# The root of 1024 moves from rstd into gamma in a routed two-layer adapter kernel

## The chip, the cores and the metric

The kernel runs on one core of a Trainium2 chip. The metric is the device time of one execution, in microseconds (us). The kernel before was timed in three runs: 2746.89 us is their median, 2745.69 the lowest and 2746.93 the highest.

## The reference

128 items of 128 rows by 1024 columns go through two adapter layers. Each item carries a role (0, 1 or 2) that picks its weights:

```
h = x @ W_down[role] + b_down[role]          # 1024 -> 512
h = gelu(h)                                  # exact gelu
y = x + h @ W_up[role] + b_up[role]          # 512 -> 1024, residual
mean, var over the 1024 columns of y
out = (y - mean) * rsqrt(var + 1e-5) * gamma[role] + beta[role]
```

The second layer does the same on the result of the first, with its own weights, gamma and beta. All of it is in fp32.

## The kernel before, in words

**Order of the items.** The kernel first sorts the items by role on the chip, so that items with the same adapter lie side by side, and pairs them: 65 pairs in each layer, 130 in all (a role with an odd number of items fills its last pair up). A pair's number is `c`. Where a pair is the first with a new adapter, new weights, biases, gamma and beta are fetched, and the weights are split in a high and a low part. The inputs hold two roles, so this happens twice in each layer: gamma and beta are fetched four times (`gains` on SyncE, lines 309 and 310).

**The step.** Every engine walks through steps `i`; in step `i` it works on several pairs at once. TensorE does the down products of pair `i` (`down`, line 517) and the seven up products of pair `i-3` (`product`, line 529), numbered 0 to 6 here as p0 to p6, in the fixed order p0, down, p1, down, ... There are 90 matmuls of 512 columns in a full step. The up product is written with sums and differences of blocks: GpSimd forms sums of the hidden blocks of pair `i-2` (`sums`, lines 470 to 475, tile `cs`), and VectorE adds the banks onto the rows in `xt` (`onto`, line 950; `last_onto`, line 958).

**Normalization.** For a pair whose rows are complete, ScalarE squares and sums (line 704), VectorE adds that up (`variance`, line 973; there H times the variance, with H = 1024, comes out, because the sum isn't divided), and GpSimd's `norm` makes `rstd` of it in two operations on a 128 by 2 tile: the power -0.5 (line 445), then, after a wait for its own first result, times the root of 1024 (line 448). Meanwhile VectorE's `scale` (line 981) computes (x + nmean) * gamma in place over 128 by 1024, once for each of the two items. ScalarE's `normal` (line 712) multiplies that by `rstd`, and GpSimd's `shift` (line 462) adds beta. Then the rows are stored. For the very last pair `norm_last` (lines 454 and 456) does one item at a time, and VectorE's `finish` (line 996) multiplies by rstd and adds beta in one operation.

**What sets the order.** Each engine's list is written by hand and runs in order; semaphores tie them. `count(eng, s, p, per, plus)` waits until semaphore `s` has `per*c + plus`. Two orders matter here. On GpSimd a step is: `sums(i-2)`, then, if pair `i-4` has a new adapter, `take_gb` (wait until gamma and beta have landed), then the semaphore `s_cg` goes up, then `norm(i-4)`, `shift(i-4, 0)`, `shift(i-4, 1)`. VectorE's `scale` waits for `s_cg`, and behind `scale` on VectorE stand, in this order, the first `last_onto` of the step (it reads the bank of p3, and TensorE's p5, which writes the same bank anew, waits for it through `s_v`), `transpose_x` in the second layer, the second `last_onto` (which waits for p4), and the rest of the step. On ScalarE `normal(i-4, 0)` stands ahead of `high_x(i+1, 0)` (line 644, the split of the next pair's x), `gelu(i, 0)` and more; each `normal` waits for `s_rs`.

The high and low parts of new weights are made by ScalarE (lines 598 and 611) and VectorE (`low_wd`, line 841; `low_wu`, line 860), in the steps just before the new gamma is first used.

## Time and profile before

| What | Value |
|---|---|
| Median of three runs | 2746.89 us (2745.69 to 2746.93) |
| Span of the profiled execution, first to last instruction | 2744.8 us |
| TensorE (PE) busy | 2683.5 us, 98% |
| VectorE (DVE) busy | 2206.7 us, 80% |
| ScalarE (ACT) busy | 1666.1 us, 61% |
| GpSimd (POOL) busy | 1385.3 us, 50% |
| Instructions | 54370 |

The profiler gives the span of the profiled execution; no other time of that execution is listed, and the span is what its rows add up to. "Idle before" is time in which the engine waited ahead of an instruction, and the arrow names what ended it; "issue" means that the profile shows nothing that the engine waited for. PEclk is the clock that TensorE was granted, 1.00 for 2.4 GHz and 0.50 for 1.2 GHz. Names such as L448 are lines of the kernel.

### The profile page before, as it was taken

Reading aid. Unit: us, or ns where it says so; the run is one execution under the profiler, and the core shown is the slowest. Engines: PE = TensorE matmul, PEld = TensorE weight load, DVE = VectorE, ACT = ScalarE, POOL = GpSimd, SP = SyncE. Lnnn points to the kernel's source line nnn. Section 1 sums busy time; section 2 is a strip of 40 time slices with the busy share of each in tenths; the row PEclk is TensorE's granted clock in tenths of the full one; section 3 lists DMA queues with packets and bytes.
Section 4 is the critical chain, followed back from the end, with each engine's and each line's share of the span. In section 5 each row is a group of like instructions: output and inputs, shape, how many; then the busy total and the mean of one; then the engine's idle time right before and its main releaser. Section 6 shows DMA issues by size and latency. Waiting matters only on the chain.

```text
span 2744.8 us, 54370 instructions
## 1 busy us (share of the span) xinstructions
PE 2683.5 (98%) x11714; PEld 2203.5 (80%) x11714; DVE 2206.7 (80%) x3357; ACT 1666.1 (61%) x2905; POOL 1385.3 (50%) x1050
## 2 busy tenths in 40 slices
PE   8999999999999999999989999999999999999997
PEld 6888888887888888888768888888778888888885
DVE  6777777779777777777898888888888888888886
ACT  5656656666666665665656566665666565665664
POOL 1455555455555555555545454554444455545545
PEclk9999999999999999999999999999999999999998
DMA  6656656666666666656766566666766665766654
GB/s 226 212 194 213 211 200 214 201 228 231 215 214 202 207 207 205 214 200 224 233 200 225 185 220 206 205 214 202 240 197 214 200 222 188 226 202 203 215 191 148
DMA packets 360590, 573.35 MB, mean 209 GB/s; under 512 B 40144, under 2 KB 239952, under 8 KB 359248
## 3 DMA queue, kind: packets, MB, share of 16 engines
q1 hardware_dynamic: 358704, 554.14, 61.6%
q10 hardware_dynamic: 1440, 15.47, 1.6%
q14 instruction: 434, 3.56, 0.5%
q8 instruction: 12, 0.20, 0.0%
HBM read 364.97 MB, written 204.47 MB: 207 GB/s over the span
## 4 chain that ended last, share of the span: by engine, by line
PE 86%; DVE 6%; issue 5%; ACT 1%; POOL 1%; DVEq 1%; DMA 0%; ACTq 0%; POOLq 0%; SPq 0%
PE pD L517 45%; PE bX L529 23%; PE bZ L529 17%; DVE wul L860 1%; DVE xt L958 1%; DVE hl L940 1%; DVE xT L911 1%; DVE xt L950 1%; DVE xt L981 0%; ACT xh L644 0%; DVE wdl L841 0%; DVE hT L925 0%; DVE xl L918 0%; POOL cs L470 0%; POOL cs L472 0%
## 5 line engine op out<-in xcount | busy, mean ns | idle before, releaser
L517 PE MATMUL pD<-wdh,xh 128*128 128x512 f32 x2080 | 812.4, 391 | 15.4 <-DVEq L902 15.4
L462 POOL TENSOR_TENSOR xt<-xt,cgb 128x1024 f32<-128x1024 f32 x258 | 630.8, 2445 | 359.4 <-ACT xt L712 359.4
L517 PE MATMUL pD<-wdh,xl 128*128 128x512 f32 x2080 | 811.3, 390 | 0.0
L517 PE MATMUL pD<-wdl,xh 128*128 128x512 f32 x2080 | 811.2, 390 | 0.0
L470 POOL TENSOR_TENSOR cs<-hT 128x256 f32<-128x256 f32 x130 | 151.6, 1166 | 902.9 <-DVE hT L925 902.9
L704 ACT ACTIVATE pC<-xt,nmean 128x512 f32<-128x512 f32 x520 | 358.7, 690 | 246.0 <-DVE nmean L966 236.8
L712 ACT ACTIVATE xt<-xt,rstd 128x1024 f32<-128x1024 f32 x258 | 296.3, 1149 | 316.3 <-POOL rstd L448 312.7
L517 PEld LDWEIGHTS pD<-wdh,xh 128*128 128x128 f32 x2080 | 391.6, 188 | 99.7 <-DVEq L902 12.4
L517 PEld LDWEIGHTS pD<-wdh,xl 128*128 128x128 f32 x2080 | 391.7, 188 | 82.1
L517 PEld LDWEIGHTS pD<-wdl,xh 128*128 128x128 f32 x2080 | 391.8, 188 | 81.3
L529 PE MATMUL bX<-wuh,hh 128*128 128x512 f32 x1040 | 408.0, 392 | 17.4 <-DVEq L902 9.5
L529 PE MATMUL bX<-wuh,hl 128*128 128x512 f32 x1040 | 406.0, 390 | 0.0
L529 PE MATMUL bX<-wul,hh 128*128 128x512 f32 x1040 | 405.9, 390 | 0.0
L694 ACT ACTIVATE hh<-cs 128x512 fp32r<-128x512 f32 x260 | 163.6, 629 | 371.8 <-PE bX L529 283.6
L940 DVE TENSOR_TENSOR hl<-cs,hh 128x512 fp32r<-128x512 f32 x260 | 298.9, 1168 | 104.0 <-issue 97.6
L981 DVE SCALAR_TENSOR_TENSOR xt<-xt,nmean,cgb 128x1024 f32<-128x1024 f32 x260 | 327.8, 1301 | 2.5 <-POOLq L483 2.4
L529 PE MATMUL bZ<-wuh,hh 128*128 128x512 f32 x780 | 307.4, 394 | 12.6 <-issue 7.6
L529 PE MATMUL bZ<-wul,hh 128*128 128x512 f32 x780 | 305.0, 391 | 0.0
L529 PE MATMUL bZ<-wuh,hl 128*128 128x512 f32 x780 | 304.9, 391 | 0.0
L950 DVE TENSOR_TENSOR xt<-bX,xt 128x512 f32<-128x512 f32 x260 | 178.8, 688 | 147.8 <-PE bX L529 146.6
L958 DVE SCALAR_TENSOR_TENSOR xt<-bX,xt 128x512 f32<-128x512 f32 x260 | 176.9, 680 | 97.9 <-PE bX L529 97.7
L445 POOL TENSOR_TENSOR rstd<-var,mhalf 128x2 f32<-128x2 f32 x129 | 218.1, 1691 | 68.5 <-DVE var L973 64.9
(106 smaller groups left out, 3817.4 us busy)
## 6 DMA issues: line engine op xcount, KB each, us to landing
xq<-in_xB SPq DMA_DIRECT2D x130, 512.0 KB, 3.6
htok<-hg SPq DMA_DIRECT2D x260, 256.0 KB, 2.9
hq<-htok SPq DMA_DIRECT2D x1040, 64.0 KB, 2.2
xt<-in_x SPq DMA_DIRECT2D x130, 512.0 KB, 4.3
mid<-xt SPq DMA_DIRECT2D x130, 512.0 KB, 3.8
xq<-mid SPq DMA_DIRECT2D x520, 128.0 KB, 3.2
xt<-mid SPq DMA_DIRECT2D x130, 512.0 KB, 4.4
out<-xt SPq DMA_DIRECT2D x128, 512.0 KB, 3.0
```

The costliest lines, as they stand in the source:

```text
L445: eng.tensor_tensor(rstd[:, n:n + 2], var[:, n:n + 2], mhalf[:, 0:1].broadcast_to([128, 2]), ALU.pow)\
L462: eng.tensor_tensor(xt[:, k, :], xt[:, k, :], cgb[:, 1, :], ALU.add).then_inc(s_o, 1)
L470: eng.tensor_tensor(cs[:, 0, :], b1, b2, ALU.add).then_inc(s_S, 1)
L517: last = eng.matmul(pD[e][:, :], a[:, e, 128 * k:128 * k + 128], w[:, k, :], start=False, stop=(k == 7 and n == 2), skip_group_check=True)
L529: last = eng.matmul(bank[:, :], a[:, left, 128 * c:128 * c + 128], w[:, n, c, :], start=(start and c == 0 and m == 0), stop=(c == 1 and m ...
L694: eng.activation(dst, src, ACT.Copy).then_inc(s_hh, 1)
L704: eng.activation(junk[:, :], xt[:, u.slot(e), K * m:K * m + K], ACT.Square, bias=nmean[:, n:n + 1], accum_out=ssq[:, b, m, e:e + 1]).then_ ...
L712: eng.activation(xt[:, k, :], xt[:, k, :], ACT.Copy, scale=rstd[:, n:n + 1]).then_inc(s_z, 1)
L940: eng.tensor_tensor(blocks, src, high.bitcast(fp32), ALU.subtract).then_inc(s_hl, 1)
L950: eng.tensor_tensor(half(u, e, m), bank[:, :], half(u, e, m), ALU.add).then_inc(s_v, 1)
L958: eng.scalar_tensor_tensor(out=half(u, e, m), in0=bank[:, :], scalar=1.0, in1=half(u, e, m), op0=ALU.mult, op1=ALU.add, accum_out=ys[:, b, ...
L981: eng.scalar_tensor_tensor(out=xt[:, k, :], in0=xt[:, k, :], scalar=nmean[:, n:n + 1], in1=cgb[:, 0, :], op0=ALU.add, op1=ALU.mult).then_i ...
```

## The change

`rstd` is no longer multiplied by the root of 1024. Instead gamma is multiplied by it once, when a new gamma has landed: GpSimd's `take_gb` multiplies the whole 128 by 1024 tile by the number, and waits until that is done before `s_cg` goes up. The counts of `s_rs` are halved, since each pair now gives one signal where it gave two, and the tile and the memset that held the root are gone.

```
-        rooth = sb("rooth", [128, 1])
+        s_gr = sem("s_gr")
...
-            eng.memset(rooth[:, :], float(H) ** 0.5).then_inc(s_id, 1)
             eng.memset(zero[:, :], 0.0).then_inc(s_zero, 1)
-            eng.wait_ge(s_id, 2)
+            eng.wait_ge(s_id, 1)
...
             def take_gb(p):
-                eng.wait_ge(s_gb, pg.next() * 32 + 32)
+                c = pg.next()
+                eng.wait_ge(s_gb, c * 32 + 32)
+                eng.sem_inc(s_seen, 1)
+                eng.tensor_scalar(cgb[:, 0, :], cgb[:, 0, :], float(H) ** 0.5, None, ALU.mult).then_inc(s_gr, 1)
+                eng.wait_ge(s_gr, c + 1)
                 eng.sem_inc(s_seen, 1)

             def norm(p):
                     eng.tensor_tensor(rstd[:, n:n + 2], var[:, n:n + 2], mhalf[:, 0:1].broadcast_to([128, 2]), ALU.pow)\
                        .then_inc(s_rs, 1)
-                    count(eng, s_rs, p, 2, 1)
-                    eng.tensor_tensor(rstd[:, n:n + 2], rstd[:, n:n + 2], rooth[:, 0:1].broadcast_to([128, 2]), ALU.mult)\
-                       .then_inc(s_rs, 1)

             def norm_last(p, e):
                 eng.tensor_tensor(rstd[:, n:n + 1], var[:, n:n + 1], mhalf[:, 0:1], ALU.pow).then_inc(s_rs, 1)
-                count(eng, s_rs, p, 2, 2 * e + 1)
-                eng.tensor_tensor(rstd[:, n:n + 1], rstd[:, n:n + 1], rooth[:, 0:1], ALU.mult).then_inc(s_rs, 1)
...
             def normal(p, e):
-                    count(eng, s_rs, p, 2, 2)
+                    count(eng, s_rs, p, 1, 1)
...
             def finish(u, e):
-                count(eng, s_rs, u, 2, 2 * e + 2)
+                count(eng, s_rs, u, 1, e + 1)
```

## Rows read from the trace of the kernel before

**Rows 1.** The page: busy time, share of span, instructions; then the chain's shares by engine.

```profile
PE 2683.5 (98%) x11714; PEld 2203.5 (80%) x11714; DVE 2206.7 (80%) x3357; ACT 1666.1 (61%) x2905; POOL 1385.3 (50%) x1050
...
PE 86%; DVE 6%; issue 5%; ACT 1%; POOL 1%; DVEq 1%; DMA 0%; ACTq 0%; POOLq 0%; SPq 0%
```

**Rows 2.** Windows: length, then busy us of each engine, granted clock, DMA share, GB/s.

```profile
1003.00:1023.40 20.40, 20.40 (x92) 16.89 (x91) 15.21 (x25) 12.55 (x23) 11.03 (x8) 1.00 0.63 208
...
668.80:699.20 30.40, 23.15 (x92) 17.73 (x91) 25.08 (x34) 17.89 (x31) 13.74 (x9) 0.94 0.45 151
```

**Rows 3.** Waits: who waited for whom, us in total, times, the longest.

```profile
ACT xt L712 <- POOL rstd L448: 312.7, 115, 7.3
...
ACT hh L694 <- issue: 26.8, 4, 7.5
```

**Rows 4.** Groups of GpSimd's lines: count, busy us, mean ns, idle before.

```profile
L445 POOL TENSOR_TENSOR rstd<-var,mhalf 128x2 f32<-128x2 f32 x129 | 218.1, 1691 | 68.5 <-DVE var L973 64.9 <-DMA cgb<-in_be 0.4
...
L448 POOL TENSOR_TENSOR rstd<-rstd,rooth 128x2 f32<-128x2 f32 x129 | 78.5, 609 | 10.1
...
L430 POOL MEMSET xt<- 128x1024 f32 x1 | 1.0, 952 | 0.0
```

**Rows 5.** Timeline of a plain step: start us, us, engine, line, what.

```profile
1013.00 2.48 DVE L981 SCALAR_TENSOR_TENSOR xt<-xt,nmean,cgb 128x1024 f32<-128x1024 f32 x2
1013.11 1.74 POOL L445 TENSOR_TENSOR rstd<-var,mhalf 128x2 f32<-128x2 f32 x1 [0.41 <-DVE var L973]
...
1014.92 0.61 POOL L448 TENSOR_TENSOR rstd<-rstd,rooth 128x2 f32<-128x2 f32 x1
...
1016.80 2.41 POOL L462 TENSOR_TENSOR xt<-xt,cgb 128x1024 f32<-128x1024 f32 x1 [1.26 <-ACT xt L712]
...
1018.26 2.03 DVE L918 TENSOR_TENSOR xl<-xq,xh 128x1024 fp32r<-128x1024 f32 x1
```

**Rows 6.** The chain that ended last, steps 30 and 31: start us, us, what.

```profile
619.60 0.63 POOL rstd L448
```

**Rows 7.** Timeline, steps 29 to 31.

```profile
600.95 2.40 POOL L462 TENSOR_TENSOR xt<-xt,cgb 128x1024 f32<-128x1024 f32 x1 [1.10 <-ACT xt L712]
...
602.03 2.40 DVE L841 TENSOR_TENSOR wdl<-rwd,wdh 128x1024 fp32r<-128x1024 f32 x1
...
632.15 1.06 ACT L644 ACTIVATE xh<-xq 128x1024 fp32r<-128x1024 f32 x1 [1.04 <-issue]
```

**Rows 8.** Timeline, step 34, which first uses the second gamma.

```profile
708.77 0.74 POOL L475 TENSOR_TENSOR cs<-hT,cs 128x256 f32<-128x256 f32 x1
...
708.91 2.87 DVE L981 SCALAR_TENSOR_TENSOR xt<-xt,nmean,cgb 128x1024 f32<-128x1024 f32 x2 [0.73 <-POOLq L483]
711.71 0.68 DVE L958 SCALAR_TENSOR_TENSOR xt<-bZ,xt 128x512 f32<-128x512 f32 x1
...
712.80 0.39 PE L529 MATMUL bZ<-wuh,hh 128*128 128x512 f32 x1
```

**Rows 9.** Timeline, step 99, which first uses the fourth gamma.

```profile
2067.60 2.47 DVE L981 SCALAR_TENSOR_TENSOR xt<-xt,nmean,cgb 128x1024 f32<-128x1024 f32 x2
2069.99 0.68 DVE L958 SCALAR_TENSOR_TENSOR xt<-bZ,xt 128x512 f32<-128x512 f32 x1
...
2071.73 0.39 PE L529 MATMUL bZ<-wuh,hh 128*128 128x512 f32 x1
```

**Rows 10.** Timeline, step 69, which first uses the third gamma.

```profile
1436.03 2.48 DVE L981 SCALAR_TENSOR_TENSOR xt<-xt,nmean,cgb 128x1024 f32<-128x1024 f32 x2 [0.17 <-POOLq L483]
1438.43 0.69 DVE L958 SCALAR_TENSOR_TENSOR xt<-bZ,xt 128x512 f32<-128x512 f32 x1
...
1441.08 0.39 PE L529 MATMUL bZ<-wuh,hh 128*128 128x512 f32 x1
```

**Rows 11.** Timeline, step 4, which first uses the first gamma.

```profile
88.29 0.69 DVE L958 SCALAR_TENSOR_TENSOR xt<-bX,xt 128x512 f32<-128x512 f32 x1 [1.39 <-PE bX L529]
```

**Rows 12.** The chain that ended last, its last microseconds: start us, us, what.

```profile
2736.62 0.20 POOL rstd L456
```

More of the change, by code:

```diff
@@ L567, in _ @@
         def _(eng):
-            eng.wait_ge(s_id, 2)
+            eng.wait_ge(s_id, 1)
             eng.activation(gelu_set[:, :], mhalf[:, :], ACT.Gelu)
```

## The prediction

> **What bounds the kernel now.** I read the page first. TensorE is busy 98% of the span and makes up 86% of the chain that ended last [rows 1]. The windows show what that means: in a plain step TensorE is busy all of the 20.40 us, at full clock, while VectorE works 15.2, ScalarE 12.6 and GpSimd 11.0 (first of [rows 2]). 130 such steps are 2652 us of the span of 2744.8. The other 93 us are the start, the drain of the last steps, and the steps in which an adapter changes: step 33 lasts 30.4 us with VectorE busy for 25.1 of them (second of [rows 2]). So an edit moves the time only there; in a plain step it must first use up the slack of its engine.
>
> The waits come next. ScalarE waits 312.7 us in 115 places for line 448, the operation that goes [rows 3]. That looks like a large sum, but these waits lie beside TensorE's 20.40 us. The chain of waits says where it is otherwise: in the stretch from 600 to 660 us the chain leaves TensorE and passes through line 448, at 619.60 and once more at 638.56, 0.63 and 0.62 us each (the first of these two stands in [rows 6]), and at the very end it passes through line 456 [rows 12]. At the other adapter changes it runs over VectorE and no operation on rstd.
>
> **What goes: the second operation on rstd.** 129 operations of 609 ns are 78.5 us of GpSimd [rows 4]. In the plain step the power ends at 1013.11 + 1.74 = 1014.85, the multiplication runs from 1014.92 to 1015.53 [rows 5]; without it rstd is ready 0.68 us sooner, in every step. ScalarE's `normal` follows, and GpSimd's add of beta (1016.80) follows that. This also clears VectorE's way: its 128x1024 subtraction began at 1018.26 and ended at 1020.29, 1.08 us after the add's end at 1019.21 [rows 5]; the one at 602.03 ended at 604.43, 1.08 us after an add that ended at 603.35 [rows 7]. VectorE stood until GpSimd's add was through, so an add that is 0.68 us earlier frees VectorE as much earlier. In a plain step all this is cover: TensorE takes 20.40 us with or without it, and I count 126 or so steps at nothing. If that cover were gone, it would be up to 0.68 us a step.
>
> Around the first big adapter change it does count. Three links are in line: the add that held up the weight work of step 29 (602.03), and line 448 in steps 30 and 31. Each is worth 0.68. One may be lost: at 632.15 ScalarE waited 1.04 us for something that the profile doesn't name [rows 7]; TensorE or a transfer. If the advance ends there, only the last 0.68 is left; if not, all three are: 2.04. I take two: **-1.36 us** (bounds -0.68 and -2.04). At the third and fourth changes (around 1400 and 2030 us) the chain doesn't pass rstd: nothing.
>
> At the end line 456 takes 0.20 us in the chain, with a handover of 0.07 as between 1014.85 and 1014.92 [rows 12, 5]: **-0.27 us**. The memset that goes and the wait for one signal less stand ahead of a start that waits for the items' roles: nothing.
>
> **What comes: gamma times the root, four times.** It is one operation of 128x1024 with one tensor as input, on GpSimd, in front of `s_cg`. VectorE's two `scale` operations wait for that, and `last_onto` and TensorE's p5 stand behind. No row shows such an operation. From below, the memset of the same size took 0.95 us [rows 4]; from above, the add with two tensor inputs took 2.41 [rows 5]. I take 1.2, near the memset, since one of the add's two operands is missing. With three handovers of 0.07, say 0.2 to 0.25, it puts 1.45 us between the end of `sums` and `scale`.
>
> On one rule the Trainium skill goes further: GPSIMD Engine Reference, section 3.1, puts a body of one or two operations per element at 1.03 cycles an element, and a body with two inputs at 2.6. By that the new operation is at the memset's end of the bracket, an estimated 0.9 us at that page's 1.2 GHz, and the sum below would be 0.6 us lower.
>
> Step by step:
> - Step 34: `sums` ended at 708.77 + 0.74 = 709.51. `scale` began at 708.91, since the signal had been sent as soon as the last sum was issued [rows 8]. Now it begins at 709.51 + 1.45 = 710.96. The pair took 2.87 beside GpSimd's sum, alone it takes 2.48 [rows 5], so `last_onto` begins at 711.71 - 0.39 + 2.05, which is 1.65 us later. TensorE's p5 began at 712.80, 0.42 after `last_onto` ended (711.71 + 0.68 = 712.39). VectorE enters this step 0.68 earlier, since its subtraction in step 33 follows an add of beta as above. 1.65 - 0.68 - 0.42 = 0.55, taken as **+0.6 us**. Bounds: 0.3 with 0.95 us, 2.4 with 2.41 us and no advance.
> - Step 99: `scale` at 2067.60 moves by 1.45; `last_onto` ended at 2070.67, p5 began at 2071.73, so 1.06 is slack [rows 9]: **+0.4 us**. Bounds 0.1 and 1.6.
> - Step 69: `scale` at 1436.03 had waited for gamma and beta; `last_onto` ended at 1439.12, p5 began at 1441.08: 1.96 of slack against 1.45 [rows 10]: nothing; 0.7 with 2.41.
> - Step 4: `last_onto` had ended and VectorE sat idle for 1.39 us until p4 was through at 88.29 [rows 11]; p5 begins one group of six matmuls later (20.40 / 15 = 1.36), so there are some 2.6 us of slack against at most 1.45: nothing, with 2.41 too (2.66).
>
> On GpSimd the power of that step comes 1.2 us later and the multiplication that goes gives half of it back. The adds of beta behind it move with it, and nothing on SyncE's queue but these two stores; ScalarE's later work in the step does wait for `normal`, but step 34's stretch up to the next step's down products has over a microsecond of room in the plain pattern. I leave it at nothing.
>
> **The sum**, against the profiled span: -1.36 - 0.27 + 0.6 + 0.4 = -0.6, so 2744.8 becomes 2744.2. The median of the runs stands 2.1 us above the span (2746.89 against 2744.8), and I keep that: **2746.3 us**.
>
> **Rivals.**
> - *Gamma's operation is dear.* It costs what the add costs, 2.41 us, and holds `s_cg` for as long. Then steps 34, 99 and 69 give 2.4 + 1.6 + 0.7 = 4.7; with the least gain, -0.68 - 0.27, it is +3.8: 2750.7 us, slower than before. Two steps pay for each microsecond, so the change loses from some 1.5 us for the operation on. For it speaks that all of GpSimd's known long operations run at that pace; against it that the memset doesn't.
> - *A first call that waits.* An operation of a kind that GpSimd hasn't run before may stand until its code is there. The nearest row is ScalarE's longest wait without a cause, 7.5 us [rows 3]. In step 4 that is 1.45 + 7.5 less the 2.6 of slack, so +6.4: 2752.7 us; if it happened at each of the four, 7.5 more in each of three, 2775. The Trainium skill names such a thing: GPSIMD Engine Reference, section 2.1, says that the first call to a freshly loaded kernel pays a load of about 6 us that no instruction shows. Nothing in the trace before shows such a gap, so I hold it for unlikely.
> - *More is freed than counted.* All three links count (-2.04), the operation takes 0.95 us (+0.3 + 0.1), and with shorter stalls TensorE keeps its clock in one stretch more. In step 33 the granted clock was 0.94 [rows 2], which is 0.06 x 30.4 = 1.8 us lost. Sum: -2.04 - 0.27 + 0.4 - 1.8 = -3.7: 2743.2 us.
> - *The power takes the time over.* The multiplication ended at 1015.53, with VectorE's second `scale` (1013.00 + 2.48 = 1015.48) [rows 5]. If rstd were held by `scale` and not by the multiplication, the gains in steps 29 to 31 would be 0, and the sum +1.2 + 0.4 - 0.27: 2748.2 us. Against it: the power ended at 1014.85, before `scale` did.
>
> **Chances and range.** The forecast, within a microsecond and a half: 0.60; the dear operation 0.14; the first call 0.04; more freed 0.12; the power takes over 0.10. The range reaches from the third rival to close to the first, 2743.4 to 2750.2. A measurement can tell about 0.2% of this kernel, 5.5 us, from no change. Only the first call lies past that on the slow side, and a sum of small misses: 0.05. On the fast side 0.03. The rest, 0.92, is no change.
>
> **What would show it.** Right: no line 448; ScalarE's wait for rstd now names line 445 and is some 0.68 x 115 = 78 us shorter than 312.7; plain steps of 20.40 us as before; four operations of about 1.2 us on cgb; a wait of about 2 us of VectorE's `scale` for GpSimd in step 34; step 34 longer than 20.40 us by half a microsecond; steps 30 to 33 together shorter by 1.4; the last finish 0.27 sooner. Wrong: a plain step that isn't 20.40 us, a gamma operation above 1.5 us, or a stall on TensorE at steps 4 or 69. What I can't see is how the pauses without a named cause on VectorE and ScalarE fall once the timing shifts; they could move the sum by a microsecond or two either way.

## The result and the profile after

The changed kernel takes 2752.12 us, the median of 20 runs (2749.16 to 2753.77). The kernel before takes 2746.64 us beside it, also 20 runs (2745.48 to 2748.84). The ratio is 1.0018, with a 95% interval of 1.0012 to 1.0024: slower by 5.5 us, where 0.6 us faster was forecast. The profiled execution has a span of 2750.7 us (own time 2752.52) against 2744.8. At 0.18% that is just inside what the prediction called no change, and 1.9 us above the upper end of its range.

First the page: busy time of each engine, share of the span, instructions; then the shares of the chain that ended last. It answers to [rows 1].

```profile
PE 2687.6 (98%) x11714; PEld 2208.4 (80%) x11714; DVE 2157.7 (78%) x3357; ACT 1675.1 (61%) x2905; POOL 1318.5 (48%) x922
...
PE 85%; DVE 6%; issue 6%; POOL 1%; ACT 1%; DVEq 1%; DMA 0%; ACTq 0%; POOLq 0%; SPq 0%
```

GpSimd has 128 instructions fewer: 129 multiplications in the steps, two for the last pair and one memset are gone, and four operations are new. It works 67 us less, not 78.5, mainly since the four new ones bring 11.1. The groups of its lines, with count, busy time, mean ns and the idle time before, show both (they answer to [rows 4]):

```profile
L448 POOL TENSOR_TENSOR rstd<-var,mhalf 128x2 f32<-128x2 f32 x129 | 219.1, 1698 | 64.5 <-DVE var L971 59.5 <-POOL cgb L440 1.2
...
L440 POOL TENSOR_SCALAR cgb<-cgb 128x1024 f32<-128x1024 f32 x4 | 11.1, 2780 | 0.2 <-DMA cgb<-in_be 0.2
```

The second row is the news: gamma's operation takes 2.78 us. The prediction took 1.2 and had 2.41 as its upper bound.

The windows of a plain step, of step 33, and of the steps 34 and 99, which first use the second and the fourth gamma (length, busy time of each engine, granted clock, DMA share, GB/s; compare [rows 2]):

```profile
1003.00:1023.40 20.40, 20.40 (x92) 16.89 (x91) 14.28 (x25) 12.69 (x24) 10.42 (x7) 1.00 0.64 218
670.08:699.65 29.57, 22.94 (x91) 17.61 (x90) 24.47 (x33) 17.93 (x31) 13.64 (x8) 0.94 0.51 167
699.80:724.10 24.30, 22.30 (x91) 17.96 (x90) 17.77 (x30) 13.00 (x23) 13.12 (x8) 0.93 0.74 237
2061.10:2084.50 23.40, 21.16 (x91) 16.64 (x90) 18.20 (x29) 11.53 (x21) 11.89 (x8) 1.00 0.71 216
...
716.00:719.40 3.40, 3.40 (x10) 2.63 (x9) 2.99 (x4) 3.40 (x6) 2.27 (x2) 0.50 0.22 87
```

The plain step is what it was, 20.40 us, all of it TensorE's. Step 33, counted from its first matmul to that of the next step, is 0.6 us shorter (29.72 after 30.36). Step 34 now lasts 24.3 us and step 99 23.4. In step 34 TensorE is idle for 2.0 us (24.30 less 22.30). It is also busy longer than in a plain step, because its granted clock stands at 0.50 for 3.4 us, from 716.0 on: at the 1.2 GHz level the same matmuls take 1.7 us more. TensorE had stood still until 715.56, just before that.

The timeline of step 34 tells the stall from its cause to its effect (start, duration, engine, line, what, and in brackets the idle time before it with what ended it; compare [rows 8]):

```profile
708.77 0.74 POOL L473 TENSOR_TENSOR cs<-hT,cs 128x256 f32<-128x256 f32 x1
...
709.47 2.78 POOL L440 TENSOR_SCALAR cgb<-cgb 128x1024 f32<-128x1024 f32 x1
...
712.41 2.48 DVE L979 SCALAR_TENSOR_TENSOR xt<-xt,nmean,cgb 128x1024 f32<-128x1024 f32 x2 [4.23 <-POOLq L481]
...
714.81 0.69 DVE L956 SCALAR_TENSOR_TENSOR xt<-bZ,xt 128x512 f32<-128x512 f32 x1
...
715.56 0.50 PE L527 MATMUL bZ<-wuh,hh 128*128 128x512 f32 x1 [2.00 <-DVE xt L956]
...
2071.54 2.78 POOL L440 TENSOR_SCALAR cgb<-cgb 128x1024 f32<-128x1024 f32 x1
...
2074.48 2.48 DVE L979 SCALAR_TENSOR_TENSOR xt<-xt,nmean,cgb 128x1024 f32<-128x1024 f32 x2 [2.84 <-POOLq L481]
...
2077.62 0.50 PE L527 MATMUL bZ<-wuh,hh 128*128 128x512 f32 x1 [1.77 <-DVE xt L956]
```

Read from the top: GpSimd's last sum, gamma's operation, VectorE's `scale` 0.16 us after that ends, then `last_onto`, then TensorE's p5. It is the chain the prediction named, and the last three rows are the same in step 99, with a stall of 1.77 us. The chain that ended last (start, duration, what) now runs over gamma's operation; before, it stayed on TensorE all through this step:

```profile
709.47 2.79 POOL cgb L440
...
715.56 2.61 PE bZ L527 x6
```

The waits (who waited for whom, total, times, longest) show the other half, which did what was forecast. They answer to [rows 3]:

```profile
ACT xt L710 <- POOL rstd L448: 239.8, 114, 6.6
...
DVE xt L979 <- POOLq L481: 13.5, 6, 4.2
```

ScalarE waits 72.9 us less for rstd. Nearly all of that lies in plain steps and is worth nothing. The second row was 2.4 us before, and its 4.23 is the wait in step 34.

To see where the time is, I cut every profile at the first matmul of chosen steps. The stretches below are us, counted from the traces; the last column is the span. Kernels of the experiments stand in the same table.

```
                    to 0  0-3   4     5-29   30-33 34    35-68  69    70-98  99    100-129 130-  span
before              17.21 58.64 20.40 510.00 92.94 20.42 707.88 20.40 609.53 21.11 612.76 53.55 2744.8
e7_prices           28.98 60.45 20.40 510.00 92.39 20.71 708.43 20.40 608.11 21.94 613.30 54.30 2759.4
e13_more_prices     29.06 58.74 20.40 510.00 92.91 20.47 707.89 20.40 608.23 21.89 613.23 53.63 2756.9
e2_gamma_only       16.91 59.56 20.49 510.00 92.31 25.43 708.26 21.40 608.65 23.21 613.09 53.20 2752.5
after               16.90 60.44 20.49 510.00 91.96 24.31 708.41 21.05 607.56 23.42 612.19 54.01 2750.7
after_again         16.93 59.47 20.49 510.00 91.46 23.17 707.87 21.28 608.09 23.33 612.75 52.76 2747.6
e1_no_gamma         16.93 59.74 20.40 510.00 91.66 20.40 708.33 20.40 608.37 21.64 612.03 53.78 2743.7
e11_two_ops         16.89 60.37 20.40 510.00 91.97 20.97 709.10 20.40 607.25 22.58 612.35 53.05 2745.3
e3_half             16.93 60.28 20.40 510.00 91.90 21.41 708.73 20.40 607.14 23.10 612.59 54.16 2747.0
e6_two_inputs       17.01 60.39 20.40 510.00 91.94 21.81 708.21 20.40 607.94 23.55 612.46 53.09 2747.2
e4_twice            16.92 60.33 25.06 510.00 91.48 27.47 708.53 27.10 607.96 28.70 612.00 52.78 2768.3
e10_root_on_dve     16.94 58.81 20.40 510.00 91.33 20.40 708.88 20.40 609.17 22.46 613.46 52.06 2744.3
e8_dve_gamma        17.57 59.73 20.40 510.75 91.41 20.40 708.76 20.40 610.71 22.44 613.43 53.88 2749.9
e14_root_in_square  16.95 58.99 20.40 510.00 91.51 20.40 708.38 20.40 607.38 21.53 612.37 53.95 2742.3
```

From before to after, the steps 4, 34, 69 and 99 cost 0.09 + 3.89 + 0.65 + 2.31 = 6.9 us. Steps 30 to 33 give back 1.0, steps 70 to 98 2.0. The first four steps take 1.8 more, but they do so by 0.1 to 1.8 us in all the kernels of the table, those without the new operation among them, so this is not the change's. What is left, stretch by stretch, is 0.6 us or less.

One profile of each kernel says little about a microsecond, and the table has a control for that. In e7_prices and e13_more_prices (both below) everything that differs from the kernel before lies ahead of the first step; from there on they are the kernel before. They have 608.1 and 608.2 in steps 70 to 98, and 21.9 in step 99. So of the 2.0 that steps 70 to 98 seem to give back, only about 0.9 is left when the four profiles with the multiplications (608.1 to 609.5) are set against the eight that lack them and add nothing on VectorE (607.1 to 608.4), and of the 2.31 of step 99 some 0.8 can be there without the change. Steps 30 to 33 are clear: 92.3 to 92.9 with the multiplications, 91.3 to 92.0 in all ten profiles without. The first four steps of the kernel before take 58.6 to 60.5; in `after` the granted clock stands at 0.50 from 12.8 to 23.0 us, in `before` from 13.2 to 20.0.

### The profile page after: what moved, and what is told of

The parts are those of the page before. It is cut to its first block, busy times and chain, and to the rows that moved or that the text cites. A ratio compares the mean times of both kernels' runs of the same rounds, so it can differ in the third digit from the quotient of the medians.

```text
span 2750.7 us, 54270 instructions
## 1 busy us (share of the span) xinstructions
PE 2687.6 (98%) x11714; PEld 2208.4 (80%) x11714; DVE 2157.7 (78%) x3357; ACT 1675.1 (61%) x2905; POOL 1318.5 (48%) x922
## 4 chain that ended last, share of the span: by engine, by line
PE 85%; DVE 6%; issue 6%; POOL 1%; ACT 1%; DVEq 1%; DMA 0%; ACTq 0%; POOLq 0%; SPq 0%
PE pD L515 45%; PE bX L527 23%; PE bZ L527 17%; DVE wul L858 1%; DVE xt L956 1%; DVE hl L938 1%; DVE xT L909 1%; DVE xt L948 0%; DVE xt L979 0%; DVE wdl L839 0%; DVE xl L916 0%; POOL cgb L440 0%; POOL cs L468 0%; ACT xh L642 0%; DVE hT L923 0%
## 5 line engine op out<-in xcount | busy, mean ns | idle before, releaser
L938 DVE TENSOR_TENSOR hl<-cs,hh 128x512 fp32r<-128x512 f32 x260 | 289.5, 1132 | 99.7 <-issue 73.5
```

Source lines behind the costliest of these rows:

```text
L938: eng.tensor_tensor(blocks, src, high.bitcast(fp32), ALU.subtract).then_inc(s_hl, 1)
```

## The experiments

Two theories were to be told apart. The first: all of the loss comes from gamma's operation at its real price, through the steps in which a new gamma arrives, while the multiplications that went brought what was forecast. The rival: leaving the multiplications out costs something too (GpSimd and VectorE shift against each other, the clock falls more often), or the steps pay for the new semaphore and wait more than for the operation. Each run stands beside the kernel before on the same chip.

**The changed kernel again.** No edit.

> The changed kernel once more, beside the variants. Expected: 1.0018 times before (2752 us against 2746.6), with gamma's operation at 2.78 us four times. If the difference is a matter of how the clock happens to fall, this ratio should come out elsewhere, near 1.000.

Measured: 2750.43 against 2747.49, ratio 1.0012 (1.0003 to 1.0022), span 2747.6. The loss repeats, smaller. In this profile TensorE stands longer in step 34 (2.47 us before p5) but has a granted clock of 1.00 all through, so the step takes 23.17 instead of 24.31. The other runs show the same: of the 20 runs of the result, 17 had a mean granted clock of 0.990 to 0.992 and took 2752.3 us on average, 3 had 0.993 or 0.994 and took 2749.3; of the 11 here, 6 took 2751.8 at the lower clock and 5 took 2749.3 at the higher. The kernel before has this too: of its 90 runs beside the experiments the 30 with 0.992 or less took 2748.2 us, the other 60 took 2746.9. So the loss is 2.4 us at the higher clock and about 4 at the lower, and the changed kernel had the lower one more often, in 23 of 31 runs against 30 of 90. That it is step 34's clock in those runs isn't shown, since only one execution of each has a profile: between the two profiles lie 3.1 us, of which 1.1 are step 34's, 1.0 the first four steps' and 1.2 those behind step 130.

**Without gamma's operation.** Only the gain is left; the root is missing from the result.

```diff
-                eng.tensor_scalar(cgb[:, 0, :], cgb[:, 0, :], float(H) ** 0.5, None, ALU.mult).then_inc(s_gr, 1)
-                eng.wait_ge(s_gr, c + 1)
-                eng.sem_inc(s_seen, 1)
```

> The changed kernel without gamma's operation and its wait: the root of 1024 is left out of the result altogether (all outputs but beta are too small by it). Theory 1 (gamma's operation in front of s_cg is the whole loss; leaving out line 448 is a small gain): 2745 us, 1 to 2 us below before, span 2743; no stall on p5 in steps 34, 69, 99. Theory 2 (the shorter rstd chain itself does harm, by moving GpSimd's adds of beta onto other VectorE work): at or above before, 2747 to 2749. Theory 3 (halved clock at the start and in the drain, whatever the edit): between 2746 and 2748, with the stalls gone but the drain still a microsecond longer.

Measured: 2745.3 against 2747.49, ratio 0.9993 (0.9984 to 1.0002), so -2.2 us, with zero in the interval. That fits the gain forecast (1.6), though the time alone doesn't prove that there is one; it does leave no room for a harm of more than 0.6 us. Steps 34, 69 and 4 are 20.40 again. Its timeline in step 34 has `scale` back where [rows 8] has it, with the wait and the 2.87 us beside GpSimd's sum:

```profile
708.10 2.87 DVE L976 SCALAR_TENSOR_TENSOR xt<-xt,nmean,cgb 128x1024 f32<-128x1024 f32 x2 [0.73 <-POOLq L478]
```

**Gamma's operation alone.** The kernel before, with both operations on rstd, and with the new operation and its wait multiplying gamma by 1.0.

```diff
-                eng.wait_ge(s_gb, pg.next() * 32 + 32)
+                c = pg.next()
+                eng.wait_ge(s_gb, c * 32 + 32)
+                eng.sem_inc(s_seen, 1)
+                eng.tensor_scalar(cgb[:, 0, :], cgb[:, 0, :], 1.0, None, ALU.mult).then_inc(s_gr, 1)
+                eng.wait_ge(s_gr, c + 1)
                 eng.sem_inc(s_seen, 1)
```

> The kernel before, with gamma multiplied by 1.0 in take_gb and waited for, and both operations on rstd kept. Theory 1: the loss without the gain: stalls on p5 of 3.5 us in step 34, 2 in step 99, 0.6 in step 69, and perhaps one more stretch at half clock (1.7): 2752.5 to 2755 us. Theory 2 (shorter chain does the harm): 2747 us.

Measured: 2753.39 against 2747.49, ratio 1.0022 (1.0013 to 1.0031): +5.9 us. The two halves add up, as far as the intervals of 2.5 us on either side can tell: -2.2 + 5.9 = +3.7, between the +2.9 of the changed kernel on the same chip and the +5.5 of the result. The rival, that leaving out the multiplications does harm, falls. In step 34:

```profile
713.02 2.48 DVE L986 SCALAR_TENSOR_TENSOR xt<-xt,nmean,cgb 128x1024 f32<-128x1024 f32 x2 [4.23 <-POOLq L488]
```

The step takes 25.43 us, 5.0 over a plain one and 2.3 more than in `after_again`. GpSimd comes to gamma 10.82 us into the step, where it was 10.14 in `after_again`: here the multiplications are still ahead of it. (The 9.68 of `after` has a second reason, told under the tensor_tensor form.) And the granted clock stands at 0.50 for 3.4 us from 717.6 on, behind the stall, which is 1.7 us.

**A price list.** Before the first step, when nothing else runs on it, GpSimd works through eight operations on gamma's tile. Each waits for the one before; the wait lines, and a memset of the tile ahead of the list, are left out here. The rest is the kernel before.

```diff
+            eng.tensor_scalar(cgb[:, 0, 0:256], cgb[:, 0, 0:256], 1.0, None, ALU.mult).then_inc(s_gr, 1)
+            eng.tensor_scalar(cgb[:, 0, 0:512], cgb[:, 0, 0:512], 1.0, None, ALU.mult).then_inc(s_gr, 1)
+            eng.tensor_scalar(cgb[:, 0, :], cgb[:, 0, :], 1.0, None, ALU.mult).then_inc(s_gr, 1)
+            eng.tensor_scalar(cgb[:, 0, :], cgb[:, 0, :], 1.0, 0.0, ALU.mult, ALU.add).then_inc(s_gr, 1)
+            eng.tensor_copy(cgb[:, 1, :], cgb[:, 0, :]).then_inc(s_gr, 1)
+            eng.tensor_tensor(cgb[:, 1, :], cgb[:, 0, :], mhalf[:, 0:1].broadcast_to([128, H]), ALU.mult).then_inc(s_gr, 1)
+            eng.tensor_scalar(cgb[:, 0, :], cgb[:, 0, :], 1.0, None, ALU.add).then_inc(s_gr, 1)
+            eng.tensor_tensor(cgb[:, 0, :], cgb[:, 0, :], cgb[:, 1, :], ALU.mult).then_inc(s_gr, 1)
...
```

> The kernel before with eight operations on GpSimd put in at its start, on the still unused gamma tile, each after the one before has ended, while VectorE is mostly on small tiles: multiplication by a constant of 128x256, 128x512 and 128x1024, two operations in one (times, plus) at 128x1024, a copy, times a broadcast column (two tensor inputs), plus a constant, and a product of two tiles. Theory 'one pass costs 2.7 ns an element': 0.75, 1.45, 2.78, about 2.8 to 3.3, and the copy about 1.0. Theory 'a fixed start of about 1.7 us and the memset's 1 ns an element': 1.95, 2.25, 2.78. The broadcast product should be at the add's 2.4.

The timeline at the start of this kernel, in the order of the edit:

```profile
3.99 0.87 POOL L435 TENSOR_SCALAR cgb<-cgb 128x256 f32<-128x256 f32 x1
4.95 1.55 POOL L437 TENSOR_SCALAR cgb<-cgb 128x512 f32<-128x512 f32 x1
6.58 2.77 POOL L439 TENSOR_SCALAR cgb<-cgb 128x1024 f32<-128x1024 f32 x1
9.44 1.05 POOL L441 TENSOR_SCALAR cgb<-cgb 128x1024 f32<-128x1024 f32 x1
10.55 1.04 POOL L443 COPY cgb<-cgb 128x1024 f32<-128x1024 f32 x1
11.67 1.89 POOL L445 TENSOR_TENSOR cgb<-cgb,mhalf 128x1024 f32<-128x1024 f32 x1
13.65 2.78 POOL L447 TENSOR_SCALAR cgb<-cgb 128x1024 f32<-128x1024 f32 x1
16.52 2.56 POOL L449 TENSOR_TENSOR cgb<-cgb 128x1024 f32<-128x1024 f32 x1
```

No rival had this. The operation with one step of arithmetic takes 2.77 us, the same with a second step (plus 0.0) 1.05 us. More work is 2.6 times as fast. One input with one step costs even more than two full inputs (2.56). As 2.77 is what it takes with the engine alone, the 2.78 in the kernel is no contention with VectorE. The first of the kind took no longer than the later ones in proportion, and in the changed kernel all four take 2.78 on average, so nothing of the first-call rival is seen. (One run, 2761.18 us; the first matmul of the steps comes 11.8 us later than before.) A broadcast column in place of the second tile brings tensor_tensor to 1.89, where 2.4 was expected.

**The two-step form in the kernel.** The same multiplication, plus 0.0.

```diff
-                eng.tensor_scalar(cgb[:, 0, :], cgb[:, 0, :], float(H) ** 0.5, None, ALU.mult).then_inc(s_gr, 1)
+                eng.tensor_scalar(cgb[:, 0, :], cgb[:, 0, :], float(H) ** 0.5, 0.0, ALU.mult, ALU.add).then_inc(s_gr, 1)
```

> The changed kernel, with gamma's operation written as times the root, plus 0.0: two operations in one instruction, which the price list gave as 1.05 us where one operation took 2.78. Theory 1 (the loss is that instruction's length in front of s_cg): the p5 stalls become 1.0 in step 34, 0.3 in step 99, 0 in step 69 and the kernel falls to 2746 us, within a microsecond of the 2746.3 forecast, at or just under before; 4.3 us less than the changed kernel. Rival (the wait and the handover cost, not the length): stays at 2750 to 2752.

Measured: 2746.36 (2743.02 to 2747.94) against 2747.46, ratio 0.9995 (0.9986 to 1.0004), so no difference from before can be told. The group of its line, and the `scale` of step 34:

```profile
L440 POOL TENSOR_SCALAR cgb<-cgb 128x1024 f32<-128x1024 f32 x4 | 4.2, 1051 | 0.1
...
710.50 2.48 DVE L979 SCALAR_TENSOR_TENSOR xt<-xt,nmean,cgb 128x1024 f32<-128x1024 f32 x2 [2.51 <-POOLq L481]
```

This is the cleanest test of the failed step: same place, same wait, same data, same multiplications gone; only the price is near the 1.2 that the prediction took. Step 34 takes 20.97, which is 0.57 over a plain step where 0.55 was forecast for 1.2 us (0.40 for 1.05), steps 69 and 4 are 20.40, as forecast, and the time is 1.1 us below before, where 0.6 was forecast. Step 99 takes 22.58, 1.5 more than before instead of 0.4. That isn't p5: TensorE's longest pause in that step is 0.91 us, 6.9 us after the step's start and far ahead of p5, and the same pause stands in the kernel before (e13_more_prices, in its step 99):

```profile
2074.70 0.50 PE L546 MATMUL bX<-wuh,hh 128*128 128x512 f32 x1 [0.92 <-DVE xt L967]
```

**Half of gamma.** The one-step form on 512 of the 1024 columns; the other half stays without the root.

```diff
-                eng.tensor_scalar(cgb[:, 0, :], cgb[:, 0, :], float(H) ** 0.5, None, ALU.mult).then_inc(s_gr, 1)
+                eng.tensor_scalar(cgb[:, 0, 0:K], cgb[:, 0, 0:K], float(H) ** 0.5, None, ALU.mult).then_inc(s_gr, 1)
```

> The changed kernel with only the first 512 columns of gamma multiplied (the other half of the outputs is too small by the root): the instruction should take 1.55 us. Theory 1: 1.2 us less in each of the steps 34 and 99, 0.9 in step 69: 3.3 us less than the changed kernel, 2747 us. Rival (wait and handover): 2750 to 2752.

Measured: 2747.09 against 2747.46, ratio 0.9997 (0.9988 to 1.0006). The operation takes 1.49 us, step 34 21.41.

```profile
L440 POOL TENSOR_SCALAR cgb<-cgb 128x512 f32<-128x512 f32 x4 | 6.0, 1494 | 0.0
```

**Twice over gamma.** A second pass by 1.0 behind the first.

```diff
-                eng.wait_ge(s_gr, c + 1)
+                eng.wait_ge(s_gr, 2 * c + 1)
+                eng.sem_inc(s_seen, 1)
+                eng.tensor_scalar(cgb[:, 0, :], cgb[:, 0, :], 1.0, None, ALU.mult).then_inc(s_gr, 1)
+                eng.wait_ge(s_gr, 2 * c + 2)
```

> The changed kernel with a second pass over gamma (times 1.0) behind the first: 2.85 us more in front of s_cg at each new gamma. Theory 1: the slack is used up everywhere by now, so each of the steps 34, 69 and 99 pays all of it (8.6 us together) and step 4, which had some, about 2.9: 2762 us, and up to 6 more if stretches at half clock come with the longer stalls. Rival (the length hardly counts): under 2755.

Measured: 2770.12 (2768.01 to 2771.89) against 2747.46, ratio 1.0081 (1.0067 to 1.0095), 2 us above the upper end of what was expected. With the slack used up the second pass is paid for in all four steps, and by more than its length: step 34 takes 27.47, 69 27.10, 99 28.70, and step 4, which hid the 2.78 but for 0.09, takes 25.06. Together that is 20.1 more than in `after_again`, for 4 x 2.78 = 11.1 of GpSimd. The windows of step 69 (as above) show the clock's share in that: 0.64 and 0.68 in ten microseconds in which the stall ends, (0.36 + 0.32) x 5 = 3.4 us of full clock at most. In step 4 (from 94.5 us), 34 (from 722.6) and 99 (from 2094.7) the clock stands at 0.50 for 3.4 us each, 1.7 us lost. With these 8.5 us taken off, 11.6 is left; the second pass ends 2.97 us after the first, and 4 x 2.97 = 11.9. So the length is paid in full, once in each of the four steps, and the rest is the clock's. The last row below is `scale` in step 34.

```profile
1455.00:1460.00 5.00, 2.92 (x7) 2.35 (x8) 4.42 (x8) 2.85 (x4) 3.17 (x2) 0.64 0.12 48
1460.00:1465.00 5.00, 5.00 (x17) 3.93 (x16) 4.71 (x7) 4.97 (x10) 2.66 (x1) 0.68 0.85 256
...
719.81 2.48 DVE L982 SCALAR_TENSOR_TENSOR xt<-xt,nmean,cgb 128x1024 f32<-128x1024 f32 x2 [7.19 <-POOLq L484]
```

**The tensor_tensor form.** Gamma times a broadcast column with the root, on GpSimd.

```diff
-                eng.tensor_scalar(cgb[:, 0, :], cgb[:, 0, :], float(H) ** 0.5, None, ALU.mult).then_inc(s_gr, 1)
+                eng.tensor_tensor(cgb[:, 0, :], cgb[:, 0, :], rooth[:, 0:1].broadcast_to([128, H]), ALU.mult).then_inc(s_gr, 1)
```

> The changed kernel with gamma multiplied by a broadcast column (two tensor inputs), an instruction that the price list gave as 1.89 us. Theory 1: between the 1.05 us instruction (2746.4) and the 2.78 us one (2750.4 to 2752.1), on the line between them: p5 stalls 1.4 in step 34, 1.1 in step 99, 0 in step 69; 2748 us. Rival (a threshold somewhere between): at one of the two ends.

Measured: 2747.2 against 2747.25, ratio 1.0001 (0.9992 to 1.001). The operation takes 1.89 us, as in the list, and step 34 21.81; the time is 0.8 us below the 2748 expected. Together with the others this gives step 34's rule. In the table: the operation's length, when it began (us into the step), what the step takes over 20.40 less what the fallen clock took, and the first two less the third.

```
               length  begins  excess, clock taken off  remainder
e11_two_ops    1.05    9.65    0.57                     10.13
e3_half        1.49    9.68    1.01                     10.16
e6_two_inputs  1.89    9.68    1.41                     10.16
after          2.78    9.68    3.91 - 1.7 = 2.2         10.3
after_again    2.78    10.14   2.77                     10.15
e2_gamma_only  2.78    10.82   5.03 - 1.7 = 3.3         10.3
```

The remainder is one number to within 0.2 us: gamma has to be through 10.1 to 10.3 us into the step, and whatever ends later is paid for in full. In the kernel before, the sums alone end at 10.3 into the step (709.51, with the step's start at 699.18), so there was no room for anything.

The column "begins" holds a second thing, which comes from TensorE and not from GpSimd. Counted from the start of step 33, GpSimd's last sum ends at 39.4 us in `after`, `after_again`, e1_no_gamma, e11_two_ops, e3_half, e6_two_inputs and e4_twice, and at 40.4 to 40.7 in the four profiles with the multiplications. What differs is when TensorE enters step 34: step 33 has one or two stretches of 3.4 us at clock 0.50, and where one begins in its last 12 us the step takes 29.4 to 29.7 us in these seven, otherwise 29.2. So the same GpSimd looks 0.5 us earlier in `after` than in `after_again`, and step 34 pays that much less. The steps 33 and 34 together, step 34's own clock taken off, are the same in both: 52.3 and 52.4.

```profile
L442 POOL TENSOR_TENSOR cgb<-cgb,rooth 128x1024 f32<-128x1024 f32 x4 | 7.6, 1889 | 0.0
```

**More prices.** What makes the second step cheap: seven operations this time (waits and memset left out as above), out of place, with other second steps, other sizes, another first step, and a column in place of the number.

```diff
+            eng.tensor_scalar(cgb[:, 1, :], cgb[:, 0, :], 1.0, None, ALU.mult).then_inc(s_gr, 1)
+            eng.tensor_scalar(cgb[:, 1, :], cgb[:, 0, :], 1.0, 1.0, ALU.mult, ALU.mult).then_inc(s_gr, 1)
+            eng.tensor_scalar(cgb[:, 1, :], cgb[:, 0, :], 1.0, 0.0, ALU.mult, ALU.max).then_inc(s_gr, 1)
+            eng.tensor_scalar(cgb[:, 0, 0:512], cgb[:, 0, 0:512], 1.0, 0.0, ALU.mult, ALU.add).then_inc(s_gr, 1)
+            eng.tensor_scalar(cgb[:, 0, 0:256], cgb[:, 0, 0:256], 1.0, 0.0, ALU.mult, ALU.add).then_inc(s_gr, 1)
+            eng.tensor_scalar(cgb[:, 1, :], cgb[:, 0, :], 1.0, None, ALU.max).then_inc(s_gr, 1)
+            eng.tensor_scalar(cgb[:, 0, :], cgb[:, 0, :], mhalf[:, 0:1], None, ALU.mult).then_inc(s_gr, 1)
...
```

> The kernel before with seven more operations on GpSimd at its start, to see what makes one operation in one instruction dear: one multiplication out of place (if writing over the input were the cause: about 1.0; else 2.78), times and times again (1.05 if any two operations take the short way), times and maximum (the same question), times plus at 128x512 and 128x256 (0.55 and 0.35 if the short way is 1 ns an element), one maximum (2.78 if every single operation is dear), and one multiplication by a column of constants rather than by a number (2.78 if the kind of operand doesn't matter).

The timeline of the list (one run, 2758.63 us):

```profile
3.98 2.78 POOL L435 TENSOR_SCALAR cgb<-cgb 128x1024 f32<-128x1024 f32 x1
6.84 1.05 POOL L437 TENSOR_SCALAR cgb<-cgb 128x1024 f32<-128x1024 f32 x1
7.97 3.65 POOL L439 TENSOR_SCALAR cgb<-cgb 128x1024 f32<-128x1024 f32 x1
11.71 0.62 POOL L441 TENSOR_SCALAR cgb<-cgb 128x512 f32<-128x512 f32 x1
12.41 0.40 POOL L443 TENSOR_SCALAR cgb<-cgb 128x256 f32<-128x256 f32 x1
12.90 2.77 POOL L445 TENSOR_SCALAR cgb<-cgb 128x1024 f32<-128x1024 f32 x1
15.77 2.85 POOL L447 TENSOR_SCALAR cgb<-cgb,mhalf 128x1024 f32<-128x1024 f32 x1
```

In or out of place makes no difference (2.78), nor does the first operation (max 2.77). Multiply-multiply is fast like multiply-add (1.05); multiply-max takes 3.65, longer than one step. So it is certain pairs that are fast, not pairs as such; which others are, these runs don't show.

**The root on VectorE, beside var.** No operation on gamma; var is multiplied by 1/H in a small operation of its own, which makes up for the root in rstd.

```diff
...
-                                              in1=ssq[:, b, 1, :], op0=ALU.add, op1=ALU.add).then_inc(s_var, 1)
+                                              in1=ssq[:, b, 1, :], op0=ALU.add, op1=ALU.add).then_inc(s_vh, 1)
+                    count(eng, s_vh, u, 1, 1)
+                    eng.tensor_scalar(var[:, 2 * b:2 * b + 2], var[:, 2 * b:2 * b + 2], 1.0 / H, None, ALU.mult).then_inc(s_var, 1)
```

> The changed kernel with no operation on gamma; VectorE multiplies the 128x2 variance by 1/1024 in an operation of its own behind the sum, before GpSimd takes the power. Computes the same. Expected: 0.25 to 0.3 us more on VectorE per step and the 0.68 us on GpSimd saved, so 0.4 net on the rstd chain: 2745.5 to 2746.5 us, between the version without gamma's operation (2745.3) and before. Rival: in the second layer VectorE has next to no slack in the steps after its loop returns, and those pay 0.3 each: 2748 to 2749.

Measured: 2746.69 against 2747.46, ratio 0.9996 (0.9987 to 1.0005). 129 more operations of 0.19 us on VectorE show in no plain step (510.00 us for steps 5 to 29). In its one profile the stretches 70 to 98 and 100 to 129 are 0.8 and 1.4 us longer than in `e1_no_gamma`; whether these operations use up what the removal brought there isn't shown, as the two times can't be told apart.

```profile
L972 DVE TENSOR_SCALAR var<-var 128x2 f32<-128x2 f32 x129 | 24.6, 191 | 4.5
```

**Gamma on VectorE.** The same operation on gamma, on VectorE, ahead of the `scale` operations of the step that first needs it.

```diff
...
+            def root_gamma(p):
+                c = pgr.next()
+                eng.wait_ge(s_gb, c * 32 + 32)
+                eng.sem_inc(s_seen, 1)
+                eng.tensor_scalar(cgb[:, 0, :], cgb[:, 0, :], float(H) ** 0.5, None, ALU.mult).then_inc(s_gr, 1)
+                eng.wait_ge(s_gr, c + 1)
+                eng.sem_inc(s_seen, 1)
...
+                kinds.when_new(u + -1, root_gamma)
```

> The changed kernel with the multiplication of gamma on VectorE, just ahead of its first scale, in place of GpSimd's. Computes the same. Theory: what counts is the time that scale is held up at each new gamma. On VectorE a 128x1024 operation with one tensor input was not in the traces; its sums with two tensor inputs take 1.2 us, so 0.6 to 1.2 plus 0.1 for the wait. VectorE starts it when gamma is there and does not wait for GpSimd's sums to end. So 0.5 to 1.2 in each of the steps 34 and 99 less slack: 2745.5 to 2746.5 us, no worse than the version with two operations in one instruction. Rival (VectorE's time is dearer than GpSimd's, since weight work is queued on it): 2747 or more.

Measured: 2750.29 against 2747.25, ratio 1.0013 (1.0004 to 1.0022). My theory had it at 2745.5 to 2746.5; the rival, that VectorE's time is the dearer, was right, and it is 3 us slower than before. The operation itself is cheap, 0.75 us on VectorE, and the steps 4, 34 and 69 have no stall. The group of `scale` says what else came:

```profile
L976 DVE TENSOR_SCALAR cgb<-cgb 128x1024 f32<-128x1024 f32 x4 | 3.0, 750 | 0.5 <-issue 0.3 <-DMA cgb<-in_be 0.2
...
L985 DVE SCALAR_TENSOR_TENSOR xt<-xt,nmean,cgb 128x1024 f32<-128x1024 f32 x260 | 326.5, 1296 | 28.1 <-issue 20.7 <-POOLq L478 5.9 <-DVE cgb L976 1.3
```

Ahead of `scale` VectorE now stands 20.7 us in "issue", that is without waiting for anything; before it was next to none (2.5 us in all, 2.4 of them for GpSimd). On 130 steps this is 0.16 us a step: the question whether the item has a new gamma is a branch that every step has to take. The time is in steps 5 to 29 (+0.75, where no gamma changes), 35 to 68, 70 to 98 (+2.3 over `e1_no_gamma`), 99 and behind. That the branch is the cause is argued from this row; no run had the branch without the operation.

**The root in ScalarE's square.** ScalarE squares (x - mean) / 32 instead of (x - mean), the root of 1024 being 32. The mean over 32 is a new operation of 128x1, and EPS stands in place of H*EPS. No operation on gamma, one on rstd.

```diff
...
+                        eng.activation(nms[:, n:n + 1], nmean[:, n:n + 1], ACT.Copy, scale=H ** -0.5).then_inc(s_ns, 1)
+                        count(eng, s_ns, u, 2, e + 1)
...
-                    eng.activation(junk[:, :], xt[:, u.slot(e), K * m:K * m + K], ACT.Square, bias=nmean[:, n:n + 1],
+                    eng.activation(junk[:, :], xt[:, u.slot(e), K * m:K * m + K], ACT.Square, bias=nms[:, n:n + 1],
+                                   scale=H ** -0.5,
...
-                    eng.scalar_tensor_tensor(out=var[:, 2 * b:2 * b + 2], in0=ssq[:, b, 0, :], scalar=H * EPS,
+                    eng.scalar_tensor_tensor(out=var[:, 2 * b:2 * b + 2], in0=ssq[:, b, 0, :], scalar=EPS,
```

> Computes the same with no operation on gamma and one on rstd: ScalarE squares (x - mean)/32 instead of x - mean, for which it first scales the 128x1 mean by 1/32 in an operation of its own, so that the sum is the variance itself. Expected if the loss was only gamma's operation in front of scale: ScalarE, busy 61% of the span, hides 260 small operations of some 0.2 us and the wait of 0.1 to 0.3 behind each, except in the drain, where the last mean and variance are in the chain (0.3 to 0.6). So 2745.5 to 2746.2 us, 0.5 above the kernel without gamma's operation (2745.3) and about a microsecond below before. Rival: ScalarE's work around the adapter changes gates VectorE's weight work, and 0.5 us more per step there costs a few microseconds: 2748 or more.

Measured: 2743.39 (2742.96 to 2745.09) against 2746.57, ratio 0.9989 (0.998 to 0.9998). It is the fastest here, 3.2 us under before, where about one was expected. Of the versions that compute the reference it alone has an interval wholly below 1, if barely. ScalarE's two rows:

```profile
L704 ACT ACTIVATION_READ_ACCUMULATOR pC<-xt,nms 128x1 f32 x520 | 97.1, 187 | 0.0
L700 ACT ACTIVATE nms<-nmean 128x1 f32<-128x1 f32 x260 | 51.1, 197 | 193.0 <-DVE nmean L967 193.0
```

260 operations of 0.2 us begin after a wait for the mean that ScalarE had anyway, and its busy share goes from 61% to 63%. Against `before` the gain is in steps 30 to 33 (-1.4) and 70 to 98 (-2.2); against the four profiles with the multiplications these are -1.1 and -1.3 on average. Why it is 2 us better than expected isn't shown.

## Why the prediction was wrong

**The bound: right.** 20.40 us of TensorE in every plain step, before and after, with GpSimd's multiplication gone or gamma's operation there. None of the 78.5 us of [rows 4] came through there.

**What goes: right in size.** Forecast -1.36 in steps 30 to 33, measured -0.98 in one profile of the changed kernel and -1.48 in the other, -1.28 without gamma's operation; all profiles with and without the multiplications lie 1.0 apart on average, inside the bounds. At the end -0.27 was forecast; the stretch behind step 130 moves by -1.5 to +0.6 between profiles and can't confirm it. The stretch that isn't in the sum: steps 70 to 98 became shorter, by 1.2 to 2.4 us against `before` but only by about 0.9 against all four profiles with the multiplications, whose own spread is 1.4. The prediction put this at nothing, as the chain doesn't pass rstd there; what brings the 0.9 isn't shown. Alone the removal is -2.2 us (e1_no_gamma, with zero in the interval) against -1.6 forecast.

**What comes: the failed step.** It is the price: "I take 1.2, near the memset, since one of the add's two operands is missing". It is 2.78 us, and more than the upper bound of 2.41 from the add. Both bounds came from other kinds of operation, and the trace before had no tensor_scalar on GpSimd at all. The assumption under the bounds, that an operation with one input costs no more than one with two, is what the price list refutes (2.77 against 2.56). The rule of the Trainium skill in GPSIMD Engine Reference, section 3.1, by which bodies of one or two operations cost the same, pointed to the low end as well: the two-step form keeps to it (1.05 us, against the 0.9 worked out from the page), the one-step form doesn't (2.78).

Put 2.78 for 1.2 into the prediction's own working and the rest follows. Between the end of the sums and `scale` there are 3.03 us; the trace has 712.41 - 709.51 = 2.90. The stall of step 34 is 3.03 + 0.60 - 0.39 - 0.68 - 0.42 = 2.14; measured 2.0, and 2.47 in `after_again`. Step 99 is 3.03 - 1.06 = 1.97; p5's stall there is 1.77, while the step became 2.31 longer. Step 69 is 3.03 - 1.96 = 1.07; measured 0.65. Step 4 is 3.03 - 2.6 = 0.4; measured 0.09. Together 5.6 against 6.9 - 1.7 = 5.2 measured. The 0.68 us by which this step's work should come sooner are there as well, if profiles are compared whose step 33 has its half clock in the same places: the last sum ends at 10.32 in `before` and 9.71 in `after`, at 10.84 in e2_gamma_only and 10.18 in `after_again`, at 10.60 in e7_prices and 9.96 in e1_no_gamma, 0.61 to 0.66 sooner each time. With the gain of 1.6 that makes 2750.9 us, 4.0 over before; measured were 5.5 and, in the second set of runs, 2.9. So the slack, the handovers and the order of the work were right, and e11_two_ops, at 1.05 us, has the forecast of this part within 0.2 us in the steps 4, 34 and 69. Step 99 is the exception: it is 1.5 longer than in `before`, but 0.6 to 0.7 longer than in the two other profiles of the kernel before, which have 21.9 there.

**The term that was missing.** Of the 3.89 us that step 34 became longer in this profile, 1.7 are its stretch at half clock. It isn't in every execution: `after_again` has none in that step. The prediction spoke of the clock only as a gain (1.8 us in step 33, in the third rival), and that one didn't come: step 33 has 0.94 before and after. The clock acted the other way: after 2 us without matmuls TensorE ran 3.4 us at 0.50.

**The rivals.** The dear operation was the true one, given 0.14 and 2750.7. It is what happened, with a larger number still; "the change loses from some 1.5 us for the operation on" holds as measured: at 1.49 us the ratio is 0.9997, at 1.89 1.0001, at 2.78 1.0012 to 1.0018. The power taking over was false: the gains in steps 30 to 33 are there. The first call was false. The range failed because its upper end was the price of another operation, taken for a ceiling.

## What to carry to other kernels

Before an operation goes onto a path that others wait for, its price has to come from a row of the very same instruction form; "fewer operands" is no bound, and a short list of candidates at the start of a kernel gives the prices in one run. A loss is found where few steps lack slack, so it is worth asking for each added operation in how many places its length is paid once its cover is used up (four here: a second 2.78 cost 20 us, 22.7 less the 2.9 of the first, of which 8.5 were the clock's). And a constant factor is cheapest in an instruction that runs anyway, on the engine that waits most: as the scale of ScalarE's square it cost 0.2 us an item beside a wait, in place of 0.61 a pair on GpSimd or 2.78 on gamma.

## What was not expected of the hardware

- On GpSimd, 128x1024 in f32: tensor_scalar with one step 2.77 to 2.85 us (multiply, add, max, number or column), with multiply-add or multiply-multiply 1.05, with multiply-max 3.65; copy 1.04; tensor_tensor with a broadcast column 1.89, with two tiles 2.56. By width the one-step form takes 0.87, 1.55 and 2.77 us for 256, 512 and 1024 columns, the fast two-step form 0.40, 0.62 and 1.05. On VectorE the one-step form took 0.75.
- After a stall of TensorE of 2.0 us in step 34 (715.56) the granted clock stood at 0.50 for 3.4 us; in another profile of the same kernel, with a stall of 2.47 us from the same cause, it stayed at 1.00. Runs with the lower mean clock were 2.9 us slower (2752.3 against 2749.3).
- VectorE's 128x1024 subtraction got shorter from a change that doesn't touch it: 1643 ns on average before, 1370 after, 35 us in all. In the plain step it ended 1.08 us after GpSimd's add of beta before [rows 5], and ends 1.09 us after it now (1022.77 + 1.34 = 1024.11, the add 1020.62 + 2.40 = 1023.02); with the add 0.68 us sooner, less of it lies beside the add. In the plain step that is no gain, since TensorE's 20.40 us stand beside it. The row of before has x129 and 211.9 us; this is the one of after:

```profile
L916 DVE TENSOR_TENSOR xl<-xq,xh 128x1024 fp32r<-128x1024 f32 x129 | 176.7, 1370 | 16.3 <-ACT xh L642 15.4 <-DVE wdl L839 0.7 <-issue 0.2
```
